# Masks of one head group added by TensorE, a bias fold in four steps, a packed ring, and new places for all instruction streams

## The chip, the cores and the metric

The kernel runs on one core of one Trainium2 chip. The metric is the device time of one execution in microseconds (us). The time of the kernel before is the median of three executions.

## The reference, cut to what matters

Two layers run one after the other on x (4 x 1024 x 512, float32) with a context of 4 x 64 x 512.

```python
# layer 0: transformer block, 16 heads of 32, note scores / (32 ** -0.5)
xn1 = ln(x, g1, be1)
x = x + mha(xn1, xn1, Wq_s.., causal=True) @ W1 + b1      # self attention, 1024 x 1024 scores, 4 batches x 16 heads
xn2 = ln(x, g2, be2)
x = x + mha(xn2, ctx, Wq_c.., causal=False) @ W2 + b2     # cross attention, 64 keys
x = x + relu(ln(x, g3, be3) @ Wf1 + bf1) @ Wf2 + bf2      # 512 -> 2048 -> 512
# layer 1: three rounds of routing weights (softmax over the sequence), a sigmoid gate and a layer norm
```

What the change touches is the causal self attention and the passage from it to the cross attention.

## The kernel before, in words

The self attention is cut into 16 head groups g (batch g // 4, four heads each), and a group into two halves c2 of 512 queries. A group needs:

- projections (`pj`, lines 55 to 57): each product is three fp32r matmuls of high and low parts; ScalarE writes the high part (`pjh`, L879), VectorE the low one (`pjl`, L1013), and DMAs (`stack`, L603) put them into the stacked operands `qs` and `ks`.
- a pass for the row maxima (`mx`): scores in rows of queries by TensorE (L766), masked and reduced by VectorE (L1027 with the mask where a tile meets the diagonal, L1031 without). `mxT` (L779) turns the maxima, `tq` (L889) writes them into a row of `qs`, and `tqd` (L609) copies this row to the other three heads by a DMA.
- the attention proper: `sc` (L809) computes 128 keys x up to 512 queries. Where a tile meets the diagonal, `low` (L1038, VectorE) adds a 128x128 mask in PSUM; then `ex` (L922, ScalarE) writes the exponentials, for the first key tile into `es`, for the others into a ring `er` of 8 slots of 512. GpSimd adds them up (L681), TensorE multiplies them with the values (`pv`, L821). Per group there are 32 `low` and 64 `ex`.
- the division: `fin` (L830, L933), `f0` to `f3d` (L613, L1047, L617, L623, L687, L628).

Seven PSUM banks are handed out in the order of the planned ends. For batches 1 to 3 a layer norm (`ld`, `st`, `nm`, `lnT`..) runs some groups ahead; its last part falls into groups 1 to 2, 5 to 6 and 9 to 10.

The order of the work on every engine is written out by hand: `order1()` gives each step a place in units of one group (place 14.3 is 30% into group 14), all steps are sorted by place, and each engine's program walks this one list. So a place decides order alone; semaphores decide the times. The places of group g come from tables with one row for each of four groups (`r = g % 4`), with special rows for groups 0 and 1. SyncE issues all DMAs, in the same order, and waits in its turn.

Into groups 14 and 15, which have no projections of a later group to compute, `order2()` puts the preparation of the cross attention: weights are loaded (`2ld`, L1175; `2kv`, L1182), split by ScalarE and VectorE (`2wh`, L1349 to L1355; `2wl`, L1418), the norm's shift is folded into a bias (`2wb`, L1251: 16 fp32 matmuls of one column, 32 passes in the trace), keys and values of the context are made (`2ck`, L1259; `2cv`, L1268), zeroes are written by GpSimd (`2z`, L1214, L1217), and the first chunk of 512 queries starts (`2ldc`, L1197; `2sh`, L1371; `2w1`). From place `CROSS_AT` on, 8 chunks of the cross attention follow with a fixed pattern, and then the third stage, whose places are counted from the end of the second.

Of the kernel before, what the change touches and what calls it, by code (L numbers as in the profile page):

```python
# [14 lines left out]
KT = 4  # L15
# [106 lines left out]
LN_LOAD = (-2.514, -2.024, -1.712, -1.56)  # L122
LN_TURN = (-2.071, -1.822, -1.573, -1.348)
CUT = (0.292, 0.27, 0.283, 0.294)
PROJ_0 = (27.2, 31.3, 37.9, 40.4)
PROJ_1 = (-1.329, -1.236, -1.109, -1.047)
PROJ = ((-1.661, -1.491, -1.269, -1.082), (-1.853, -1.456, -1.346, -1.171), (-1.872, -1.647, -1.316, -1.202), (-1.958, -1.475, -1.34, -1.21))
PROJ_LONG = (0.067, 0.08, 0.146, 0.146)
VALUES_0 = (40.2, 52.3, 66.7, 68.9)
VALUES = ((-1.149, -0.992, -0.719, -0.081), (-1.444, -1.08, -0.796, -0.377))  # L130
VALUES_LONG = 0.1
MAX_0 = -0.007
MAX_1 = (-0.809, -0.507, -0.024)
MAX = ((-1.031, -0.726, -0.051), (-1.012, -0.739, -0.002), (-1.033, -0.705, -0.043), (-0.988, -0.72, -0.05))


def order1():
# [19 lines left out]
    for b in range(1, NB):  # L157
        for qt in range(4):
            t += ln_times(b, qt, 4 * b + LN_LOAD[qt], 4 * b + LN_TURN[qt])
    for g in range(16):  # L160
        r = g % 4
        cut = CUT[r]
        at = [at0(a) for a in PROJ_0] if g == 0 else [g + a for a in (PROJ_1 if g == 1 else PROJ[r])]
        for c2 in range(2):
            for wq in range(2):
                n = 2 * c2 + wq
                t += proj_times(g, c2, wq, at[n], at[n] + (0.05 if g < 2 else PROJ_LONG[r]))
                back = g - 2 + (CUT[(g - 2) % 4] if n == 0 else CUT[(g - 2) % 4] + (1 - CUT[(g - 2) % 4]) * 0.54 if n == 1 else 1) + 0.03
                t.append((at[n] + 0.1 if g == 0 else max(at[n] + PROJ_LONG[r] + 0.07, back), ("stack", g, c2, wq)))
        if g % 2 == 0:  # L170
            for sp in range(4):
                s, d = (at0(VALUES_0[sp]), 0.05) if g == 0 else (g + VALUES[r // 2][sp], VALUES_LONG)
                t += spread(s, s + d, [(("vm", g // 2, sp, i), 1) for i in range(4)])
                t.append((s + d, ("ve", g // 2, sp)))
        m0, m1, end = (at0(46), at0(54), MAX_0) if g == 0 else [g + a for a in (MAX_1 if g == 1 else MAX[r])]
# [54 lines left out]
CROSS_AT = 16.793  # L230
CROSS_LOAD = (14.019, 14.431, 14.754, 14.309, 15.318)
CROSS_SPLIT = (14.581, 14.853, 15.576)
CROSS_ONCE = (14.168, 15.027, 14.983, 15.099, 14.261, 15.089, 15.146, 14.946)
CROSS_KEYS = (15.173, 15.19, 15.199, 15.461, 15.405)
CROSS_0 = (15.723, 15.776, 15.812, 16.19)


def order2():
# [5 lines left out]
    t = list(zip(CROSS_ONCE, (("2kc",), ("2kb",), ("2wb",), ("2bw",), ("2z", 2), ("2z", 0), ("2z", 1), ("2cd",))))  # L244
# [102 lines left out]
def program(nc, A, out):  # L347
    top = ExitStack()
    with top:
# [89 lines left out]
        Q.useA, Q.useP, Q.useM, Q.useS, Q.outS, Q.slot, Q.pv = {}, {}, {}, {}, {}, {}, {}  # L439
        for s in O1:  # L440
# [10 lines left out]
            if s[0] == "sc" and s[3]:  # L451
                Q.slot[s[1:]] = len(Q.slot)
            if s[0] == "pv":
                for i in range(4):
                    Q.pv[s[1:] + (i,)] = len(Q.pv)
        Q.slot_of = {at: k for k, at in Q.slot.items()}

# [16 lines left out]
        s_sao, s_rcp, s_rec, s_low = sem("s_sao"), sem("s_rcp"), sem("s_rec"), sem("s_low")  # L474

# [59 lines left out]
        def x_rows(b, qt, i):  # L535

            return Q.xr[:, i, :] if b else Q.v[:, 2 * qt + i, :]

# [95 lines left out]
        def pool1(e, w):  # L634
# [6 lines left out]
            for s in O1:  # L641
# [28 lines left out]
                elif s[0] == "pv" and s[3]:  # L670
                    _, g, c2, j = s
                    off = max(0, 128 * (j - 4 * c2))
                    for i in range(4):
                        at = Q.slot[g, c2, j, i]
                        es, er = Q.esum[c2][i][:, off:512], Q.er[:, at % 8, off:512]
# [13 lines left out]
        def pe1(e, w):  # L689
# [10 lines left out]
            for s in O1:  # L700
# [95 lines left out]
                elif s[0] == "sc":  # L796
# [10 lines left out]
                    if par:  # L807
                        w.wait_ge(d_oh1, 16)
                    t = e.matmul(ps[:, off:512], Q.ks[par][0:100, i, 128 * j:128 * j + 128],  # L809
                                 Q.qs[par][0:100, i, 512 * c2 + off:512 * c2 + 512], start=True, stop=True)  # L810
                    t.then_inc(s_fillS.sem, 1)
                elif s[0] == "pv":
                    _, g, c2, j = s
                    nj, off = 4 * c2 + 4, max(0, 128 * (j - 4 * c2))
                    for i in range(4):
# [3 lines left out]
                        src = Q.er[:, Q.slot[g, c2, j, i] % 8, :] if j else Q.esum[c2][i][:]  # L819
                        h = 128 * (g % 2) + 32 * i  # L820
                        e.matmul(bank[BO][32 * i:32 * i + 32, off:512], values(g)[:, j, h:h + 32], src[:, off:512],  # L821
# [11 lines left out]
        def act1(e, w):  # L833
            w.wait_ge(d_cols, 16)
            for s in O1:
# [21 lines left out]
                elif s[0] == "nm":  # L857
# [4 lines left out]
                                 scale=sm[:, 104 + i:105 + i]).then_inc(s_nrm.sem, 1)  # L862
                elif s[0] == "lnh":
# [37 lines left out]
                elif s[0] == "ex":  # L901
                    _, g, c2, j, i = s
                    off, n = max(0, 128 * (j - 4 * c2)), 2 * g + c2
                    if j >= 4 * c2:
                        w.wait_ge(s_low, 32 * g + 4 * j + i + 1)
                    else:
                        w.wait_ge(s_fillS, Q.useS["sc", g, c2, j, i] + 1)
                    if j:
                        at = Q.slot[g, c2, j, i]
                        dst = Q.er[:, at % 8, off:512]  # L910
                        if at >= 8:
                            w.wait_ge(s_add, at - 7)
                            w.wait_ge(s_pv, Q.pv[Q.slot_of[at - 8]] + 1)
# [331 lines left out]
        def pe2(e, w, s):  # L1245
            if s[0] == "2wb":
                freeK(w, 0)
                w.wait_ge(d_raw2[1], 64)
                for m in range(4):
                    for k in range(KT):  # L1250
                        t = e.matmul(bank[0][:, m:m + 1], R.raw[1][:, k, 128 * m:128 * m + 128], col("be2", k), start=k == 0, stop=k == 3)  # L1251
                t.then_inc(s_fillK.sem, 1)
# [930 lines left out]
```

## Time and profile before

| | |
|---|---|
| time, median of 3 (lowest to highest) | 2273.32 us (2270.26 to 2276.59) |
| profiled execution, its own time | 2272.72 us |
| its span in the trace | 2270.9 us |
| mean granted TensorE clock | 0.984 of full speed |
| PE (TensorE) busy | 2161.4 us, 95% of the span |
| VectorE, ScalarE, GpSimd busy | 61%, 38%, 41% |

Group g of the self attention can be told in the trace by the copy of its result at its end (L929): group 9 is about 583 to 635 us, group 10 635 to 692, group 13 796 to 848, group 14 848 to 906, group 15 906 to 970. The cross attention lasts to about 1420 us, the third stage to the end. In part 2 of the page each digit is a fortieth of the span, 57 us, about one group. A busy PE is not PE at its peak: a matmul whose clock is halved is busy for twice as long.

### The profile page before, as it was taken

How to read it: one execution, taken by the hardware profiler on the slowest of the kernel's cores; microseconds unless marked ns; L12 is line 12 of the kernel's file. 1: busy time of each engine (PE TensorE's matmuls, PEld its weight loads, DVE VectorE, ACT ScalarE, POOL GpSimd, SP SyncE). 2: the span in 40 equal slices, each digit the busy share in tenths (PEclk: the TensorE clock that was granted, in tenths of full speed). 3: DMA queues.
4: the chain of work that ended last, by engine and by line, in shares of the span. 5: the costliest groups of instructions: out<-in, count | busy, mean ns of one | idle time of the engine just before them, and what ended most of it. 6: DMA issues, size and time to landing. Idle time of an engine off the chain costs nothing.

```text
span 2270.9 us, 32174 instructions
## 1 busy us (share of the span) xinstructions
PE 2161.4 (95%) x11590; PEld 1604.5 (71%) x11590; DVE 1395.7 (61%) x3349; ACT 868.7 (38%) x1610; POOL 932.4 (41%) x943
## 2 busy tenths in 40 slices
PE   7999999999999998889999998999999999999996
PEld 5666666666656664467777776888887887888784
DVE  5577766876786676456666677543455636455546
ACT  4156555655565555534333433221221222121213
POOL 1068767777777778643333342101020202111112
PEclk9999999999999997999999999999999999999998
DMA  7655555555564564211122121320112121121101
GB/s 234 78 82 97 93 85 87 106 89 83 91 111 76 82 96 126 71 56 56 56 70 77 63 80 42 121 84 24 61 61 82 53 74 66 65 66 56 42 33 47
DMA packets 106324, 177.34 MB, mean 78 GB/s; under 512 B 18335, under 2 KB 23455, under 8 KB 106161
## 3 DMA queue, kind: packets, MB, share of 16 engines
q1 hardware_dynamic: 106164, 175.29, 33.1%
q8 instruction: 91, 1.49, 0.3%
q14 instruction: 69, 0.56, 0.1%
HBM read 83.67 MB, written 40.13 MB: 55 GB/s over the span
## 4 chain that ended last, share of the span: by engine, by line
PE 81%; DVE 7%; ACT 5%; issue 3%; POOL 2%; DMA 1%; SPq 0%; POOLq 0%; ACTq 0%; DVEq 0%
PE psum L55 19%; PE psum L56 18%; PE psum L57 18%; PE psum L821 6%; PE psum L766 6%; PE psum L809 5%; PE psum L724 1%; DVE psum L1027 1%; ACT sx L1377 1%; PE psum L830 1%; PE psum L743 1%; PE psum L1327 1%; DMA small<-es 1%; PE psum L1319 1%; PE psum L1268 1%
## 5 line engine op out<-in xcount | busy, mean ns | idle before, releaser
L681 POOL TENSOR_TENSOR es<-es,er 128x512 f32<-128x512 f32 (+3 forms) x640 | 588.0, 959 | 258.4 <-PE psum L821 243.6
L922 ACT ACTIVATE er<-psum 128x512 f32<-128x512 f32 (+3 forms) x640 | 278.4, 471 | 285.6 <-DVE psum L1038 176.2
L1027 DVE CUSTOM_DVE_ANT_0 psum<-psum,mask_ts 128x384 f32<-128x384 f32 (+3 forms) x512 | 249.4, 502 | 152.9 <-PE psum L766 150.6
L766 PE MATMUL psum<-ks,qs 96*128 96x512 f32 (+3 forms) x768 | 260.4, 371 | 7.4 <-DVE mx L1027 3.5
L809 PE MATMUL psum<-qs,ks 100*128 100x512 f32 (+3 forms) x768 | 252.0, 365 | 10.6 <-DVE mx L1027 5.1
L1876 ACT ACTIVATE fy<-psum,cols 128x512 f32<-128x512 f32 x128 | 88.2, 689 | 451.9 <-PE psum L57 451.4
L766 PEld LDWEIGHTS psum<-ks,qs 96*128 96x128 f32 x768 | 139.7, 191 | 115.2 <-issue 32.9
L1031 DVE TENSOR_REDUCE mx<-psum 128x1 fp32r<-128x512 f32 x256 | 175.6, 686 | 61.0 <-PE psum L766 60.0
L55 PE MATMUL psum<-fh,hh 128*128 128x512 f32 x512 | 201.0, 393 | 7.1 <-DVE hl L1977 7.1
L55 PE MATMUL psum<-fah,fh 128*128 128x512 f32 x512 | 202.9, 396 | 0.0
L1975 DVE CAST hh<-fy 128x512 fp32r<-128x512 f32 x128 | 61.2, 478 | 228.5 <-ACT fy L1876 228.1
L57 PE MATMUL psum<-fah,fl 128*128 128x512 f32 x512 | 200.1, 391 | 0.0
L56 PE MATMUL psum<-fal,fh 128*128 128x512 f32 x512 | 199.9, 390 | 0.0
L57 PE MATMUL psum<-fh,hl 128*128 128x512 f32 x512 | 199.4, 389 | 0.0
L56 PE MATMUL psum<-fl,hh 128*128 128x512 f32 x512 | 199.3, 389 | 0.0
L809 PEld LDWEIGHTS psum<-qs,ks 100*128 100x128 f32 x768 | 143.5, 194 | 58.3 <-DVE mx L1027 17.6
L1242 POOL TENSOR_TENSOR pp<-pp,small 128x1024 f32<-128x1024 f32 x32 | 61.2, 1912 | 265.9 <-DVE small L1507 265.9
L1772 POOL TENSOR_TENSOR et<-et,vpb 128x512 f32<-128x512 f32 x24 | 35.5, 1477 | 284.9 <-ACT et L1902 284.9
L1038 DVE TENSOR_TENSOR psum<-psum,mask_st 128x128 f32<-128x128 f32 x512 | 138.3, 304 | 22.7 <-PE psum L809 21.8
L821 PE MATMUL psum<-er,v 128*32 128x512 f32 (+3 forms) x1280 | 138.5, 488 | 0.7 <-ACT er L922 0.4
L55 PEld LDWEIGHTS psum<-fh,hh 128*128 128x128 f32 x512 | 96.1, 188 | 28.8 <-DVE hl L1977 9.3
L57 PEld LDWEIGHTS psum<-fah,fl 128*128 128x128 f32 x512 | 96.3, 188 | 20.6
(260 smaller groups left out, 4588.7 us busy)
## 6 DMA issues: line engine op xcount, KB each, us to landing
qs<-stage SPq DMA_DIRECT2D x96, 256.0 KB, 5.7
ks<-stage SPq DMA_DIRECT2D x96, 256.0 KB, 8.3
rs<-rs_d SPq DMA_DIRECT2D x32, 256.0 KB
sa_d<-rs SPq DMA_DIRECT2D x32, 256.0 KB, 2.1
sx<-sa_d SPq DMA_DIRECT2D x8, 1024.0 KB, 5.7
xt<-in_x SPq DMA_DIRECT2D x32, 256.0 KB, 6.0
x_d<-xt SPq DMA_DIRECT2D x32, 256.0 KB, 2.0
fw<-in_Wf SPq DMA_DIRECT2D x16, 512.0 KB, 5.3
```

The source lines that it names most:

```text
L55: e.matmul(dst, lh, rh, start=start, stop=False)
L56: e.matmul(dst, lh, rl, start=False, stop=False)
L57: return e.matmul(dst, ll, rh, start=False, stop=stop)
L681: e.tensor_tensor(es, es, er, ALU.add).then_inc(s_add.sem, 1)
L766: t = e.matmul(bank1(*s)[:, v * wd:v * wd + wd], Q.qs[par][0:96, i, 128 * ti:128 * ti + 128], Q.ks[par][0:96, i, c0:c0 + wd], start=True, ...
L809: t = e.matmul(ps[:, off:512], Q.ks[par][0:100, i, 128 * j:128 * j + 128], Q.qs[par][0:100, i, 512 * c2 + off:512 * c2 + 512], start=True, ...
L821: e.matmul(bank[BO][32 * i:32 * i + 32, off:512], values(g)[:, j, h:h + 32], src[:, off:512], start=j == 0, stop=j == nj - 1).then_inc(s_p ...
L922: e.activation(dst, bank1("sc", g, c2, j, i)[:, off:512], ACT.Exp, scale=SCALE).then_inc(s_freeS.sem, 1)
L1027: t = e.tensor_tensor_reduce(out=ps, in0=ps, in1=mask_ts[:, 512 - wd:512], scale=1.0, scalar=-3e38, op0=ALU.add, op1=ALU.max, accum_out=mx ...
L1031: e.tensor_reduce(mx[:, at:at + 1], bank1(*s)[:, 0:wd], AX, ALU.max).then_inc(s_red.sem, 1)
L1038: e.tensor_tensor(ps, ps, mask_st[:], ALU.add).then_inc(s_low.sem, 1)
L1876: e.activation(y[:], ring3(("h", c, m)), ACT.Relu, bias=col("bf1", m), scale=1.0).then_inc(s_r3.sem, 1)
```

## The change

Five things are changed.

1. In group 14 (`MASKED_BY_PE`) VectorE adds no masks for `ex`. Instead, after each of the 32 score matmuls of the diagonal TensorE multiplies the unit matrix with a copy of the mask (`mask_r`, fp32r, in the place of the value weights, which are no longer needed) into the same 128 columns. `ex` then waits for TensorE and not for VectorE. One ScalarE step (`mkr`, at 13.78) makes the copy.
2. The bias fold `2wb` becomes four steps with places 0.034 apart.
3. The ring `er` has the same 4096 elements, but a piece takes only as many as it has columns (512, 384, 256 or 128); `freed_by` gives the last piece that lay there.
4. The tables have twelve rows: groups 0 to 3, groups 4 to 11 (two by two), groups 12 to 15.
5. The places are new. The max pass of every group is some 0.073 later; projections, layer norm and values are moved by under 0.12, those of group 0 by up to 3.7 us on its own scale; the cuts of groups 14 and 10 differ. The weight splits of the cross attention are 0.129 and 0.085 earlier, their first load 0.119 later, `CROSS_AT` is 0.149 earlier, the first chunk 0.016 later.

```diff
-PROJ_1 = (-1.329, -1.236, -1.109, -1.047)
...
-VALUES = ((-1.149, -0.992, -0.719, -0.081), (-1.444, -1.08, -0.796, -0.377))
...
-MAX_1 = (-0.809, -0.507, -0.024)
-MAX = ((-1.031, -0.726, -0.051), (-1.012, -0.739, -0.002), (-1.033, -0.705, -0.043), (-0.988, -0.72, -0.05))
+LN_LOAD = ((-2.516, -2.026, -1.714, -1.561), (-2.557, -2.032, -1.746, -1.568), (-2.517, -2.027, -1.83, -1.563))
+CUT = (0.292, 0.27, 0.283, 0.294, 0.292, 0.27, 0.283, 0.295, 0.292, 0.27, 0.317, 0.294)
...
+MAX = ((-0.985, -0.652, 0.023), (-0.735, -0.433, 0.05), (-0.966, -0.596, 0.031), (-0.914, -0.646, 0.024),
+       (-0.957, -0.652, 0.023), (-1.01, -0.666, 0.071), (-0.959, -0.631, 0.031), (-0.914, -0.646, 0.037), ...
+       (-0.959, -0.565, 0.108), (-0.919, -0.646, 0.024))
+def row(g, n=4):
+    return g if g < n else n + g % n if g < 3 * n else g - n
+MASKED_BY_PE = (14,)
...
-CROSS_AT = 16.793
-CROSS_LOAD = (14.019, 14.431, 14.754, 14.309, 15.318)
-CROSS_SPLIT = (14.581, 14.853, 15.576)
-CROSS_KEYS = (15.173, 15.19, 15.199, 15.461, 15.405)
-CROSS_0 = (15.723, 15.776, 15.812, 16.19)
+CROSS_AT = 16.644
+CROSS_LOAD = (14.138, 14.447, 14.77, 14.325, 15.345)
+CROSS_SPLIT = (14.452, 14.768, 15.491)
+CROSS_FOLD = 0.034
+CROSS_KEYS = (15.174, 15.191, 15.2, 15.432, 15.406)
+CROSS_0 = (15.739, 15.792, 15.83, 16.206)
...
-                if s[0] == "sc" and s[3] >= 4 * c2 :
+                if s[0] == "sc" and s[3] >= 4 * c2 and g not in MASKED_BY_PE:
                     t += [(a + 0.014, ("low", *s[1:])), (a + 0.028, ("ex", *s[1:]))]
                 elif s[0] == "sc":
                     t.append((a + 0.001, ("ex", *s[1:])))
...
+    t.append((MASKED_BY_PE[0] - 0.22, ("mkr",)))
...
+        for at, (g, c2, j, i) in Q.slot_of.items():
+            width = 512 - max(0, 128 * (j - 4 * c2))
+            pos = 0 if pos + width > 4096 else pos
+            under = [n for n, (lo, hi) in held.items() if lo < pos + width and pos < hi]
+            Q.freed_by[at] = max(under, default=None)
...
-                                 Q.qs[par][0:100, i, 512 * c2 + off:512 * c2 + 512], start=True, stop=True)
+                                 Q.qs[par][0:100, i, 512 * c2 + off:512 * c2 + 512], start=True, stop=not diag)
+                    if diag:
+                        w.wait_ge(s_mkr, 1)
+                        t = e.matmul(ps[:, off:off + 128], identr[:], mask_r(), start=False, stop=True)
...
+                elif s[0] == "mkr":
+                    w.wait_ge(s_const, 6)
+                    w.wait_ge(s_fillA, Q.useA["vm", 7, 3] + 1)
+                    e.activation(mask_r(), mask_st[:], ACT.Copy).then_inc(s_mkr.sem, 1)
...
+                if j == 2:
+                    w.wait_ge(s_fillS, read(MASKED_BY_PE[-1], 1, 1))
```

## Rows read from the trace of the kernel before

**Rows 1.** The page, parts 1, 2, 4 and 5.

```profile
PE 2161.4 (95%) x11590; PEld 1604.5 (71%) x11590; DVE 1395.7 (61%) x3349; ACT 868.7 (38%) x1610; POOL 932.4 (41%) x943
...
PEclk9999999999999997999999999999999999999998
...
PE 81%; DVE 7%; ACT 5%; issue 3%; POOL 2%; DMA 1%; SPq 0%; POOLq 0%; ACTq 0%; DVEq 0%
...
L922 ACT ACTIVATE er<-psum 128x512 f32<-128x512 f32 (+3 forms) x640 | 278.4, 471 | 285.6 <-DVE psum L1038 176.2 <-PE psum L809 89.5 <-POOL es L681 9.5
```

**Rows 2.** Busy time of each engine by group, then granted clock, DMA share, GB/s.

```profile
424.00:479.00 55.00, 52.55 (x321) 33.86 (x321) 44.21 (x152) 35.13 (x72) 40.39 (x47) 1.00 0.57 106
...
583.00:635.00 52.00, 51.84 (x329) 34.86 (x329) 38.54 (x126) 30.49 (x66) 40.26 (x45) 1.00 0.57 90
635.00:692.00 57.00, 53.99 (x325) 35.30 (x324) 44.85 (x154) 35.76 (x73) 41.40 (x49) 0.97 0.55 107
...
848.00:906.00 58.00, 51.91 (x246) 28.35 (x246) 39.79 (x132) 33.30 (x71) 47.88 (x48) 0.79 0.55 132
906.00:970.00 64.00, 57.81 (x257) 29.25 (x255) 30.85 (x73) 36.76 (x80) 41.48 (x39) 0.90 0.19 63
```

**Rows 3.** The same view, short stretches of groups 14 and 15.

```profile
875.00:880.00 5.00, 3.81 (x15) 1.24 (x13) 3.99 (x11) 4.22 (x8) 5.00 (x5) 0.80 0.35 114
880.00:885.00 5.00, 4.93 (x14) 2.68 (x10) 3.69 (x11) 1.14 (x3) 5.00 (x5) 0.50 0.27 91
...
890.00:895.00 5.00, 2.88 (x13) 1.46 (x13) 3.34 (x10) 3.97 (x10) 5.00 (x7) 0.66 0.24 82
...
900.00:905.00 5.00, 5.00 (x31) 4.61 (x31) 0.00 (x0) 0.19 (x1) 5.00 (x2) 0.50 0.00 0
...
950.00:960.00 10.00, 6.60 (x23) 3.35 (x19) 7.12 (x9) 4.89 (x9) 6.46 (x5) 0.51 0.46 177
```

**Rows 4.** ScalarE's waits in group 14: us in total, times, longest.

```profile
ACT er L922 <- DVE psum L1038: 13.0, 12, 3.4
```

**Rows 5.** Busy time of the masks (L1038) in groups 9 and 14.

```profile
583.00:635.00 52.00, 8.45 (x32) 1.00 0.57 90
...
848.00:906.00 58.00, 9.13 (x33) 0.79 0.55 132
```

**Rows 6.** PE in order of time: the fold; the start's fold; four matmuls of 128 columns.

```profile
896.64 6.99 PE L1251 MATMUL psum<-cols,raw 128*128 128x1 f32 x32
...
60.74 0.95 PE L733 MATMUL psum<-cols,er 128*128 128x1 f32 x8
...
600.66 0.49 PE L779 MATMUL psum<-ident,mx 128*100 128x128 f32 x4
```

**Rows 7.** GpSimd in order of time, group 14.

```profile
873.02 18.69 POOL L681 TENSOR_TENSOR es<-es,er 128x512 f32<-128x512 f32 x16
...
899.53 3.52 POOL L1217 MEMSET kbh<- 128x4096 f32 x1
902.98 3.52 POOL L1217 MEMSET kbl<- 128x4096 f32 x1
```

**Rows 8.** DMAs of group 14: count, KB each, median us to landing.

```profile
raw<-in_W SPq DMA_DIRECT2D x7, 256.0 KB, 2.9
```

**Rows 9.** TensorE's weight loads, what they waited for in group 15.

```profile
PEld psum L809 <- DVE W2l L1418: 2.5, 2, 2.1
```

**Rows 10.** The chain of waits, pieces in order of time: start, us, what.

```profile
851.73 9.33 DMA small<-es
...
947.26 5.48 DMA sx<-sa_d
...
980.06 3.40 PE psum L1286 x16
```

**Rows 11.** Group 9 in order of time: the copy of the maxima, the first score of the second half.

```profile
586.79 0.71 SPq L609 DMA_DIRECT2D qs<-qs  x1
...
598.43 0.39 PE L809 MATMUL psum<-qs,ks 100*128 100x512 f32 x1
```

More of the change, by code:

```diff
@@ L158, in order1 @@
         for qt in range(4):
-            t += ln_times(b, qt, 4 * b + LN_LOAD[qt], 4 * b + LN_TURN[qt])
+            t += ln_times(b, qt, 4 * b + LN_LOAD[b - 1][qt], 4 * b + LN_TURN[b - 1][qt])
     for g in range(16):
-        r = g % 4
+        r = row(g)
         cut = CUT[r]
-        at = [at0(a) for a in PROJ_0] if g == 0 else [g + a for a in (PROJ_1 if g == 1 else PROJ[r])]
+        at = [at0(a) for a in PROJ_0] if g == 0 else [g + a for a in PROJ[r]]
         for c2 in range(2):
@@ L243, in order2 @@
     at2 = lambda n: X0 + T * n if n < 28 else E + 0.82 * T * (n - 28)
-    t = list(zip(CROSS_ONCE, (("2kc",), ("2kb",), ("2wb",), ("2bw",), ("2z", 2), ("2z", 0), ("2z", 1), ("2cd",))))
+    t = [(CROSS_ONCE[2] + CROSS_FOLD * m, ("2wb", m)) for m in range(4)]
+    t += list(zip(CROSS_ONCE[:2] + CROSS_ONCE[3:], (("2kc",), ("2kb",), ("2bw",), ("2z", 2), ("2z", 0), ("2z", 1), ("2cd",))))
     for k in range(KT):
@@ L438, in program @@
         O1 = [s for _, s in O1]
-        Q.useA, Q.useP, Q.useM, Q.useS, Q.outS, Q.slot, Q.pv = {}, {}, {}, {}, {}, {}, {}
+        Q.useA, Q.useP, Q.useM, Q.useS, Q.outS, Q.slot, Q.pv, Q.low = {}, {}, {}, {}, {}, {}, {}, {}
         for s in O1:
@@ L452, in program @@
                 Q.slot[s[1:]] = len(Q.slot)
+            if s[0] == "low":
+                Q.low[s[1:]] = len(Q.low)
             if s[0] == "pv":
@@ L456, in program @@
         Q.slot_of = {at: k for k, at in Q.slot.items()}
+        Q.piece, Q.freed_by, held, pos = {}, {}, {}, 0
+        for at, (g, c2, j, i) in Q.slot_of.items():
[3 more added lines that the diff above has]
+            Q.freed_by[at] = max(under, default=None)
+            for n in under:
+                lo, hi = held.pop(n)
+                if hi > pos + width:
+                    held[n] = pos + width, hi
+            Q.piece[at] = slice(pos, pos + width)
+            pos += width
+            held[at] = Q.piece[at].start, pos
         d_rows, d_ct0, d_wv0, d_wt0, d_wg0, d_out0 = (sem(n) for n in ("d_rows", "d_ct0", "d_wv0", "d_wt0", "d_wg0", "d_out0"))
@@ L474, in program @@
         s_sao, s_rcp, s_rec, s_low = sem("s_sao"), sem("s_rcp"), sem("s_rec"), sem("s_low")
+        s_mkr = sem("s_mkr")
         def stk(par, w, c2):
@@ L537, in x_rows, with mask_r, exps @@
             return Q.xr[:, i, :] if b else Q.v[:, 2 * qt + i, :]
+        def mask_r():
+            return Q.W["v"][0][:, 0, 0:128]
+        def exps(at):
+            return Q.er[:].rearrange("p a n -> p (a n)")[:, Q.piece[at]]
         def raw1(j):
@@ L674, in pool1 @@
                         at = Q.slot[g, c2, j, i]
[L675 removed]
+                        es, er = Q.esum[c2][i][:, off:512], exps(at)
                         if j == 1:
@@ L818, in pe1 @@
                         w.wait_ge(s_sao, 2 * g + c2)
-                        src = Q.er[:, Q.slot[g, c2, j, i] % 8, :] if j else Q.esum[c2][i][:]
+                        src = exps(Q.slot[g, c2, j, i]) if j else Q.esum[c2][i][:]
                         h = 128 * (g % 2) + 32 * i
-                        e.matmul(bank[BO][32 * i:32 * i + 32, off:512], values(g)[:, j, h:h + 32], src[:, off:512],
+                        e.matmul(bank[BO][32 * i:32 * i + 32, off:512], values(g)[:, j, h:h + 32], src,
                                  start=j == 0, stop=j == nj - 1).then_inc(s_pv.sem, 1)
@@ L903, in act1 @@
                     off, n = max(0, 128 * (j - 4 * c2)), 2 * g + c2
-                    if j >= 4 * c2:
-                        w.wait_ge(s_low, 32 * g + 4 * j + i + 1)
+                    if j >= 4 * c2 and g not in MASKED_BY_PE:
+                        w.wait_ge(s_low, Q.low[g, c2, j, i] + 1)
                     else:
@@ L909, in act1 @@
                         at = Q.slot[g, c2, j, i]
[L910 to L913, printed above, removed]
+                        dst, last = exps(at), Q.freed_by[at]
+                        if last is not None:
+                            w.wait_ge(s_add, last + 1)
+                            w.wait_ge(s_pv, Q.pv[Q.slot_of[last]] + 1)
                         else:
@@ L1246, in pe2 @@
             if s[0] == "2wb":
[L1247 to L1252, printed above, removed]
+                m = s[1]
+                if m == 0:
+                    freeK(w, 0)
+                    w.wait_ge(d_raw2[1], 64)
+                for k in range(KT):
+                    t = e.matmul(bank[0][:, m:m + 1], R.raw[1][:, k, 128 * m:128 * m + 128], col("be2", k), start=k == 0, stop=k == 3)
+                if m == 3:
+                    t.then_inc(s_fillK.sem, 1)
             elif s[0] == "2ck":
```

30 lines of the change are left out of this document (16 added, 14 removed).

## The prediction

> **What bounds the kernel now.** I read the page first. TensorE (PE) is busy for 95% of the span and the chain that ended last is PE for 81% [rows 1], so time can only come from PE's idle time, from PE work that goes, or from its clock. The granted clock is full nearly everywhere: the digits show one 7 in the sixteenth slice, which is group 14 [rows 1]. The busy time by group says where that sits. Group 9 has PE busy for 51.84 of 52 us with VectorE at 38.5; group 6 and its twin group 10, where a layer norm of the next batch is prepared, have 52.55 of 55 and 53.99 of 57; group 14 has 51.91 of 58 at a mean clock of 0.79, and group 15 57.81 of 64 at 0.90 [rows 2]. Group 14 has 246 matmuls where group 9 has 329, and takes 6 us more [rows 2]. So ordinary groups have nothing to give, and two stretches have: 14 and 15.
>
> A mean clock of 0.79 over 58 us is 0.21 x 58 / 0.5 = 24.4 us at half speed; 0.90 over 64 us is 12.8 us [rows 2]. The short stretches show how it comes. From 875 to 880 PE is busy for 3.81 of 5 us and the clock falls; at half speed PE is then busy for 4.93 of 5, it idles again (2.88 of 5 at 890), and for 900 to 905 it is full of work at half speed while VectorE does nothing [rows 3]. What PE waits for there is VectorE: ScalarE's exponentials stood 13.0 us for the masks, once for 3.4 us [rows 4], and VectorE serves 9.13 us of masks [rows 5] beside the maxima and eight splits of W1 and Wq_c. The block that fills 900 to 905 is the bias fold, 32 passes in one piece of 6.99 us [rows 6].
>
> By the Trainium skill ("TensorE: Matmul & The Clock Gate", Part 1) the slow clock is the state after idleness and work releases it. The trace agrees so far: the clock fell behind 3.81 busy of 5 us. The same section says that the gate's observation runs free of the program, so the place of a fall can differ between runs; then part of my clock terms would be luck. This changes no term, it is why I don't take the clock terms in full.
>
> **The change part by part.**
>
> *Masks in group 14.* VectorE loses 32 masks; group 9 prices 32 at 8.45 us [rows 5]. PE gets 32 matmuls of 128 columns. Four of that form take 0.49 us with their tail [rows 6]; without it I take 0.11 each, 3.5 us. Bounds: 3.9 us by the full row, and nothing if all fall into the 58 - 51.91 = 6.1 us in which PE idles now [rows 2]. I take 3.5. In return the chain score, mask, exponential loses its middle link, so banks come free earlier. Of the 6.1 us of PE idle I take half away: -3 (bounds 0 and -6). `mkr` is one small ScalarE step on an engine with 24 of 58 us free [rows 2]; the value projection that it waits for is placed 0.17 groups (9 us) before it: 0, with 1 us as the upper bound.
>
> *Clock in group 14.* In its 24.4 us at half speed PE is busy for about 85% (4.93, 2.88 and 5.00 of 5 us [rows 3], mean 0.85): 20.8 us, which would be 10.4 at full speed. The fold is part of this: at full clock 8 passes take 0.95 us [rows 6], four steps 3.8 us instead of 6.99, and between them scores can go to VectorE, which idles throughout the block [rows 3]. I take 80% of 10.4: -8.3 (bounds 0 and -10.4).
>
> Is another engine next? GpSimd is busy for 47.88 us in group 14 [rows 2], but 7.04 of it are two memsets behind the last sum [rows 7] that nobody needs for the next few us. 40.8 us remain, so GpSimd allows the group some 8 to 10 us. The W1 loads are placed later and their splits earlier: the last load is at 14.438, its split at 14.572, 0.134 groups or 7 us, against 2.9 us to landing [rows 8]. That fits if SyncE isn't held by the division's steps just before it; if it is, ScalarE stands with the exponentials behind it, 2 us at most by the same row less the slack, taken as 0. Group 14 in sum: -3 - 8.3 + 3.5 = -7.8.
>
> *Group 15.* Scores stood 2.5 us for W2's low parts [rows 9], because a bank is shared with them; the W2 split is 0.085 groups (4.6 us) earlier: -1.5 (0 to -2.5). The new wait of its third weight split, for the scores of group 14, stands 0.49 groups behind them: 0. Its 12.8 us at half speed cost PE work of about 0.66 x 10 + 2.8 = 9.4 us, so 4.7 us at most [rows 2, 3]. But the fall at 950 lies beside the first load of `sx`, 5.48 us on the chain [rows 10], which still waits for the context's values; these are placed only 0.029 groups earlier. I take a third: -1.5. Sum -3.
>
> *The passage to the cross attention.* `CROSS_AT` 0.149 earlier looks like 8 us and is worth nothing: the first chunk's steps keep their own places, the last of its query projection ends before 16.65, and nothing of group 15 but the division's last steps stands after that. The same steps are in the same order, and chunks 1 to 7 and stage three move as one piece. The normalisation before the first transposes of 980 us [rows 10] has no PE work to cover it before or after. 0 (-2 to +1).
>
> *The ring.* The pieces of the diagonal need 3072 of 4096 elements instead of 12 of 8 slots. ScalarE waits for GpSimd's sums for 9.5 us in the whole kernel [rows 1], mostly with PE busy. -0.5 (0 to -2).
>
> *The places of groups 0 to 13.* The max pass of each group is 0.073 groups (4 us) later against the scores. Group 9's PE is at 99.7% [rows 2], so such a group can only lose. In groups 2, 6 and 10 the layer norm's steps of VectorE now meet another part of the max pass; group 10 takes 2 us more than its twin and has a clock of 0.97 [rows 2], and it alone of them gets a later place for nothing but its loads (-1.83 for -1.712). I take -1.5 for group 10 and 0 for the rest (bounds -5 and +20, see the third rival). Start of the kernel: moves of up to 3.7 us on PE's own full queue, 0 (-2 to +2).
>
> Sum: -7.8 - 3 - 0.5 - 1.5 = -12.8, against the profiled execution's 2272.7 us (span 2270.9 and 1.8 around it): 2259.9. The median of the runs is 0.6 us above the profiled one: 2260.5, said as 2260.
>
> **The rivals.**
>
> *A: as above,* 2251 to 2266.
>
> *B: the clock falls anyway.* For: VectorE keeps 30 us in group 14 with the splits, now closer together, each 128x512; the `sx` load stays; 40.8 us of GpSimd in order; ScalarE has the splits' copies too. Then group 14 gains only the waits less the masks and some 3 us of clock: -3 + 3.5 - 3 - 1.5 (W2) = -4: 2269. Against: the longest waits of rows 4 are the masks themselves.
>
> *C: slower, by the later max pass.* The maxima of the second half end now 4 us later, up to 0.071 of a group inside the group that needs them. Place: the row copy L609 ahead of the first score of the second half. In group 9 it is issued at 586.79 and that score starts at 598.43, 11.6 us later [rows 11]. 4 us later, 7.7 remain, and a small DMA in this queue took 9.33 us in group 14 [rows 10]. That is 1.6 us of PE idle, which group 10 shows to be enough for a fall of the clock (57 for 55 us [rows 2]). Since groups repeat, 1.6 us in each of 13 is +21, net +8: 2281. It decides above 1 us per group. Against: the 9.33 us come from large transfers queued ahead; they don't move, so a copy issued later would wait less behind them.
>
> *D: more.* Clock kept in both groups in full and the layer norm groups relieved: -10.4 - 6 + 0 (masks inside idle time) - 4.7 - 2.5 - 3 = -27: 2246.
>
> *E: the change is what it says but without effect,* as groups 14 and 15 are held by GpSimd: that is B with less, 2272.
>
> **How the numbers follow.** 0.3% is 6.8 us: faster means below 2266.5, slower above 2280. A 0.60, B 0.15, C 0.12, D 0.08, E 0.05. Faster takes A but for a small part, D and a third of B: 0.57 + 0.08 + 0.05 = 0.70. Slower is C above 2280 and some B and C mixed, 0.09; the same 0.21. The range leaves out most of C and half of D: 2247 to 2275.
>
> **What would show it.** Right: clock digits of 9 or so in group 14's slice and a mean over 0.9 there; group 14 at 50 us, group 15 at 61; L1038 with 480 instructions; the fold as four pieces of about 1 us; ordinary groups within 0.2 us of 52, 55, 54 and 50. Wrong by B: half-speed stretches of 10 us still in group 14. Wrong by C: ordinary groups longer by one and the same amount, PE idle ahead of L809 at the start of the second half. The prediction fails if groups 1 to 13 together move by more than 5 us either way, or if the cross attention, which I hold to be the same, changes.

## The result, and the profile after

The changed kernel takes 2283.86 us (median of 4 runs, 2283.49 to 2285.35) against 2272.61 us of the kernel before in the same series: a ratio of 1.0049 with a 95% interval of 1.0034 to 1.0064, some 11 us slower. The forecast was 2260 us, 0.6% faster, in a range of 2247 to 2275: the sign is wrong, and the range was missed.

The page of the changed kernel, the parts that answer to [rows 1]:

```profile
PE 2165.1 (95%) x11622; PEld 1608.7 (71%) x11622; DVE 1401.3 (61%) x3317; ACT 866.9 (38%) x1611; POOL 931.4 (41%) x943
...
PEclk9999999999999997899999999999999999999998
```

ScalarE's exponentials in the groups by line (columns as in part 5 of the page):

```profile
L965 ACT ACTIVATE er<-psum 128x512 f32<-128x512 f32 (+3 forms) x640 | 278.4, 472 | 260.8 <-DVE psum L1081 158.6 <-PE psum L845 90.9 <-PE psum L849 6.0
```

The 32 added matmuls and the 32 masks that went are there. ScalarE's waits for GpSimd's sums fell from 9.5 us to 2.6 (too little for this line), and its idle time here fell from 285.6 to 260.8 us. Still the span is 10.8 us longer. TensorE's slices 16 and 17 have clock digits of 7 and 8 where before only one stood out.

I take the end of each half from the copy `sao<-psum` that ScalarE makes of its accumulators.

| stretch | before, us | after, us | difference |
|---|---|---|---|
| group 0 ends at | 160.8 | 158.4 | -2.4 |
| groups 1 to 13 | 687.1 | 691.6 | +4.5 |
| group 14 | 57.8 | 51.5 | -6.3 |
| group 15, first half | 16.6 | 32.6 | +16.0 |
| group 15, second half | 47.7 | 47.3 | -0.4 |
| what follows | | | -0.6 |

The loss sits in the first half of group 15. The busy times of groups 14 and 15, and of ten microseconds at their seam (columns as in [rows 2]):

```profile
850.00:902.00 52.00, 45.92 (x256) 25.61 (x255) 35.01 (x97) 33.26 (x71) 39.55 (x41) 0.86 0.61 141
902.00:981.00 79.00, 65.86 (x283) 36.57 (x281) 42.23 (x85) 37.10 (x81) 47.74 (x42) 0.81 0.18 59
902.00:912.00 10.00, 4.53 (x20) 4.15 (x18) 10.00 (x10) 0.05 (x1) 7.91 (x5) 0.50 0.22 59
```

Group 14 does what was hoped: VectorE has 35.01 us where it had 39.79, and the clock is 0.86 for 0.79. In group 15 the clock is 0.81 for 0.90, which over the longer stretch is 30 us at half speed for 12.8. In the ten microseconds VectorE is busy all the time with ten instructions, ScalarE does nothing, and TensorE has work for 4.53 us at half clock. What VectorE does there, in order of time:

```profile
899.11 0.70 DVE L1070 CUSTOM_DVE_ANT_0 psum<-psum,mask_ts 128x512 f32<-128x512 f32 x1 [0.22 <-PE psum L801]
899.73 0.14 DVE L1070 DVE_READ_ACCUMULATOR2_ANT mx<- 128x1 fp32r x1
899.73 11.74 DVE L1476 COPY pp<-ctc 128x256 f32<-128x256 f32 x8
911.39 0.68 DVE L1074 TENSOR_REDUCE mx<-psum 128x1 fp32r<-128x512 f32 x1
911.99 0.69 DVE L1070 CUSTOM_DVE_ANT_0 psum<-psum,mask_ts 128x512 f32<-128x512 f32 x1
```

Eight copies of the context, which take 0.28 us each when nothing holds them, last 11.74 us, and the first of them alone 10.33 us. No step of mine contains them. GpSimd beside them:

```profile
897.33 1.29 POOL L722 TENSOR_TENSOR rs<-sao,rs 128x512 f32<-128x512 f32 x1
898.58 4.44 POOL L716 TENSOR_TENSOR es<-es,er 128x256 f32<-128x256 f32 x8
902.94 3.52 POOL L1260 MEMSET kbh<- 128x4096 f32 x1
906.39 3.52 POOL L1260 MEMSET kbl<- 128x4096 f32 x1
```

GpSimd's instructions stand end to end until 909.91, and the first copy ends at 910.06. And TensorE (L1295 is the fold, L845 the scores, L814 the transposition of the maxima):

```profile
904.83 1.70 PE L1295 MATMUL psum<-cols,raw 128*128 128x1 f32 x8
912.12 0.79 PE L845 MATMUL psum<-qs,ks 100*128 100x512 f32 x1 [5.59 <-DVE mx L1074]
913.01 0.93 PE L814 MATMUL psum<-ident,mx 128*100 128x128 f32 x4
```

The two last maxima of the second half stand behind the copies on VectorE; the bank of one of them and the transposition of all of them stand behind these, and TensorE, which takes its steps in the order of the list, stands 5.59 us. Its clock is at half from 901.0 to 924.9; the fall came before TensorE stood still, so this stall did not begin it. Two lines of the waits between 896 and 940 us (us in total, times, longest) say the same for the other engines:

```profile
ACT es L965 <- DVE psum L1081: 11.1, 1, 11.1
...
PE psum L845 <- DVE mx L1074: 5.8, 2, 5.6
```

In the kernel before, the same copies took 3.19 us:

```profile
895.29 3.19 DVE L1429 COPY pp<-ctc 128x256 f32<-128x256 f32 x8
```

There GpSimd had a gap from 896.9 to 899.1 us, and the first copy (1.78 us) ended at that moment; its two memsets [rows 7] came at 899.53.

### The profile page after: what moved, and what is told of

Its sections match the earlier page's. It is cut to its first block, busy times and chain, and to the rows that moved or that the text cites. A ratio compares the mean times of both kernels' runs of the same rounds, so it can differ in the third digit from the quotient of the medians.

```text
span 2281.7 us, 32057 instructions
## 1 busy us (share of the span) xinstructions
PE 2165.1 (95%) x11622; PEld 1608.7 (71%) x11622; DVE 1401.3 (61%) x3317; ACT 866.9 (38%) x1611; POOL 931.4 (41%) x943
## 4 chain that ended last, share of the span: by engine, by line
PE 82%; DVE 6%; ACT 4%; issue 3%; DMA 2%; POOL 2%; SPq 0%; POOLq 0%; ACTq 0%; DVEq 0%
PE psum L55 19%; PE psum L56 18%; PE psum L57 18%; PE psum L801 6%; PE psum L860 6%; PE psum L845 5%; PE psum L759 1%; PE psum L869 1%; ACT sx L1424 1%; PE psum L1372 1%; PE psum L778 1%; PE psum L1364 1%; PE psum L1313 1%; DVE psum L1070 1%; ACT pT L1451 1%
## 5 line engine op out<-in xcount | busy, mean ns | idle before, releaser
L965 ACT ACTIVATE er<-psum 128x512 f32<-128x512 f32 (+3 forms) x640 | 278.4, 472 | 260.8 <-DVE psum L1081 158.6
L845 PE MATMUL psum<-qs,ks 100*128 100x512 f32 (+3 forms) x768 | 250.3, 366 | 16.1 <-DVE mx L1074 6.7
L845 PEld LDWEIGHTS psum<-qs,ks 100*128 100x128 f32 x768 | 143.0, 193 | 68.4 <-issue 12.6
L1081 DVE TENSOR_TENSOR psum<-psum,mask_st 128x128 f32<-128x128 f32 x480 | 128.6, 302 | 28.2 <-PE psum L845 27.8
```

The lines of the kernel that those rows point to most:

```text
L965: e.activation(dst, bank1("sc", g, c2, j, i)[:, off:512], ACT.Exp, scale=SCALE).then_inc(s_freeS.sem, 1)
L1081: e.tensor_tensor(ps, ps, mask_st[:], ALU.add).then_inc(s_low.sem, 1)
```

## The experiments

Theory H: VectorE's copies from SBUF to SBUF stand until GpSimd lets them in; the shorter group 14 brings them there while GpSimd is still in its sums with the memsets behind, and what stands behind the copies decides the price. Rivals: R, the fold in four pieces and the denser splits let the clock fall; M, the new places of groups 0 to 13 (the later max pass, rival C of the prediction). A ratio is that of a kernel's time to the time of the kernel before in the same series, with its 95% interval in brackets. Losses and gains below are differences of ratios times 2273 us, unless a profiled execution is named. With ten runs each such a difference is good to some 3 or 4 us either way.

**The copies on ScalarE, all else as changed.**

```diff
 # in scalar's step list, was in vector's
+elif s[0] == "2cd":
+    w.wait_ge(d_ct2, 16); stacked(w)
...
-    e.tensor_copy(dst[:, :, j, :], R.ct[:, k, :]...).then_inc(s_cd.sem, 1)
+    e.activation(dst[:, :, j, :], R.ct[:, k, :]..., ACT.Copy).then_inc(s_cd.sem, 1)
```

> The changed kernel, with the eight copies of the context (pp<-ctc) at the same place but on ScalarE instead of VectorE. Theory 1 (the loss is the copies on VectorE, which stand as long as GpSimd works without a gap): 11.7 us on VectorE become eight copies of some 0.4 us on ScalarE, the first half of group 15 falls from 32.6 us to 17 to 19, the half-speed stretch of 24 us behind it goes, and the time is 2268 to 2272, 12 to 16 us less than the changed kernel and slightly under the kernel before. Rival 1 (the first half of group 15 is long because the fold's steps and the masks' passes meet a slow clock): nothing moves, 2284. Rival 2 (the new places of groups 1 to 13 are the loss): 2284 less 2 at most.

Measured: 2275.65 us (10 runs), ratio 1.0013 [1.0000, 1.0025]: 8.2 us of the 11 come back, less than the 12 to 16 expected, and the kernel is still 3.0 us behind the kernel before. TensorE is at half clock from 906.4 to 916.7 us, 10 us for 24. The copies now take 0.41 us each beside the same GpSimd work, and the first half of group 15 takes 22.8 us instead of 32.6 (16.6 before):

```profile
901.92 2.56 ACT L1417 ACTIVATE pp<-ctc 128x256 f32<-128x256 f32 x8
```

**The memsets moved instead of the copies.** Behind the first four sums of group 15 in the changed kernel, and, in the kernel before, ahead of the last four sums of group 14.

```diff
-CROSS_ONCE = (14.168, 15.027, 14.983, 15.115, 14.261, 15.112, 15.146, 14.959)
+CROSS_ONCE = (14.168, 15.027, 14.983, 15.115, 14.261, 15.2, 15.205, 14.959)
 # kernel before
-CROSS_ONCE = (14.168, 15.027, 14.983, 15.099, 14.261, 15.089, 15.146, 14.946)
+CROSS_ONCE = (14.168, 15.027, 14.983, 15.099, 14.261, 14.965, 14.966, 14.946)
```

> The changed kernel, with GpSimd's two memsets of kbh and kbl (3.52 us each) behind the first four sums of group 15 instead of ahead of them. Theory 1: GpSimd has a gap once group 14's sums are done at about 903, so the first copy ends there and not at 910; the copies take about 5 us in all, the first half of group 15 gives back 6 to 10 us, and the time is 2274 to 2278, unless the keys of the context now wait for the zeroes. Rival 1: nothing before 915 us changes, 2284.

> The kernel before, with the same two memsets ahead of the last four sums of group 14. Nothing of the change is in it. Theory 1: the copies, which begin at 895.3, now meet GpSimd without a gap until the memsets and the sums behind them are done at about 905: the first copy takes 8 to 11 us instead of 1.8, the masks behind it on VectorE come late, and the first half of group 15 or the end of group 14 is 5 to 12 us longer: 2278 to 2285, the loss of the change without the change. Rival 1: the copies keep their 3.2 us and the time its 2273.

The first gave 2285.32 us (one run). The copies fell to 1.82 us as H says, but the time did not: a new wait came for the buffer that is now zeroed too late,

```profile
ACT kbh L1409 <- POOL kbl L1260: 9.7, 1, 9.7
```

so this run shows the release of the copies and nothing on their price. The second gave 2273.88 us (one run; the runs of the kernel before beside it lie between 2270.29 and 2278.58), no loss that one run can show where 5 to 12 us were expected, though its copies were held as long as those of the changed kernel:

```profile
892.47 11.67 DVE L1429 COPY pp<-ctc 128x256 f32<-128x256 f32 x8
904.06 0.29 DVE L1038 TENSOR_TENSOR psum<-psum,mask_st 128x128 f32<-128x128 f32 x1
```

TensorE beside and behind them:

```profile
893.83 6.99 PE L1251 MATMUL psum<-cols,raw 128*128 128x1 f32 x32
900.75 0.65 PE L821 MATMUL psum<-er,v 128*32 128x128 f32 x6
904.71 0.64 PE L821 MATMUL psum<-er,v 128*32 128x128 f32 x2 [3.31 <-ACT er L922]
```

Here H's price failed while its mechanism held. Behind the copies stands a mask, not a maximum, and beside them TensorE is in the undivided fold, which waits for nobody; it idles 3.31 us, and group 14 takes 59.8 us for 57.8. So a stall of 10 us need not cost 10 us: its price is set by what waits behind it, and by how much work TensorE has meanwhile.

**The masks of group 14: given back to VectorE, and as the only edit.**

```diff
 # changed kernel
-MASKED_BY_PE = (14,)
+MASKED_BY_PE = ()
 # kernel before, alone
+MASKED_BY_PE = (14,)
...
+                    if diag:
+                        t = e.matmul(ps[:, off:off + 128], identr[:], mask_r(), start=False, stop=True)
```

> The changed kernel without its first part: group 14's masks are added by VectorE again, all places and the rest of the change as they are. Theory 1: VectorE has 8.5 us more work in group 14, which is then 54 to 58 us instead of 51.5; it comes to the copies later, when GpSimd may or may not be at the memsets, so the first half of group 15 is anything from 17 us (GpSimd idle) to 30. Time 2272 to 2290. Rival 1 (the masks' passes are themselves the cost): under 2280 with a short first half of group 15.

> The kernel before with the first part of the change alone: group 14's masks by TensorE, all places, the ring and the fold as before. Theory 2 (the masks part is a gain, since the changed kernel without it was 8 us slower): VectorE's 8.5 us go, group 14 falls from 57.8 to 50 to 54 us, group 15 stays near 64, as VectorE comes to the context's copies only after its maxima; time 2264 to 2270. Rival (the 8 us came only from where the clock fell): 2270 to 2276.

The first: 2292.17 us (4 runs), 1.0077 [1.0060, 1.0094], 6 us slower than the changed kernel. The masks by TensorE are a gain, and the slower group 14 doesn't avoid the stall either: its GpSimd work is later too (copies 907.53 to 916.90 us). The second: 2276.31 us (10 runs), 1.0014 [1.0005, 1.0024], slower than before. Group 14 falls from 57.8 to 47.4 us and the first half of group 15 rises from 16.6 to 28.3:

```profile
891.71 15.58 DVE L1448 COPY pp<-ctc 128x256 f32<-128x256 f32 x8
907.21 0.68 DVE L1437 TENSOR_TENSOR Wq_cl<-psum,Wq_ch 128x512 fp32r<-128x512 f32 x1
```

The first copy takes 14.17 us, up to 905.88; GpSimd's second memset ends at 905.7. This one part of the change alone, on the old places, makes the stall. Neither expectation held.

TensorE in the same run (L1268 is the fold, L819 the scores):

```profile
892.25 3.90 PE L1268 MATMUL psum<-cols,raw 128*128 128x1 f32 x32
907.94 1.54 PE L819 MATMUL psum<-qs,ks 100*128 100x512 f32 x3 [9.39 <-DVE Wq_cl L1437]
```

Here no maximum stands behind the copies; the last one was done at 890.5. TensorE stands 9.39 us for a PSUM bank that the split of Wq_c behind the copies must read first. The fold is undivided as in the run with the early memsets, but it met the full clock, took 3.90 us for 6.99, and was over at 896.2, so it covered less. That this is what makes the one stall dear and the other cheap is read from the two traces; no run isolates it.

**The copies on ScalarE without and with the masks, on the kernel before.**

```diff
 # control: only "2cd" from vector's to scalar's steps
 # both: the same and
+MASKED_BY_PE = (14,)
```

> The kernel before with the copies of the context on ScalarE and nothing else, the control of e10. There the first copy stood for only 1.8 us and VectorE had an idle time of 6.4 us right behind: Theory 1: 2271 to 2274, no change. Rival (the copies on VectorE always cost): under 2269.

> The kernel before with two edits: group 14's masks by TensorE (as in e5, 2276.3 us) and the copies of the context on ScalarE. In e5 the copies held VectorE for 15.6 us, and group 14 took 47.4 us and group 15 76.8 (57.8 and 64.3 in the kernel before). Theory 1: without the stall group 15 is back at 64 to 66, the two groups take 112 to 116 us for 122, and the time is 2263 to 2268: faster than both kernels. Rival (the gain of group 14 is only work put off into group 15): 2272 to 2276.

The control gave 2272.87 us (10 runs), 0.9996 [0.9984, 1.0009]: the move itself is worth nothing that can be measured in the kernel before. Both together gave 2268.29 us (12 runs), 0.9975 [0.9962, 0.9987], 8.9 us better than the masks alone. It beats both kernels and is the best of this study, at the slow end of the 2263 to 2268 expected. Its groups 14 and 15 take 51.0 and 64.6 us:

```profile
852.00:903.00 51.00, 47.14 (x268) 28.41 (x268) 29.56 (x83) 34.31 (x77) 43.54 (x44) 0.90 0.58 146
903.00:968.00 65.00, 58.43 (x258) 29.82 (x258) 31.16 (x74) 37.40 (x82) 45.28 (x41) 0.90 0.19 62
```

**Other places for VectorE's copies in the changed kernel.**

```diff
-CROSS_ONCE = (14.168, 15.027, 14.983, 15.115, 14.261, 15.112, 15.146, 14.959)
+CROSS_ONCE = (14.168, 15.027, 14.983, 15.115, 14.261, 15.112, 15.146, 15.026)
 # and, in the other kernel, 14.90
```

> The changed kernel with the copies still on VectorE but behind the last maxima of group 15 (place 15.026 for 14.959). They will still stand until GpSimd's memsets end, some 8 us. Theory 1b (the stall costs what stands behind it: in the changed kernel two maxima, whose transposition holds TensorE's queue; in e3, with nothing behind, a stall of 9.5 us cost 1 us): the transposition is done before, only masks wait; 3 to 8 us less than the changed kernel, 2276 to 2281. Theory 1a (every stall of the copies costs the same): 2284.

> The changed kernel with the copies still on VectorE but earlier, at 14.90 for 14.959, so some 4 us sooner. Theory 1 (a copy stands until GpSimd has a gap, not until the instruction at hand ends): the first copy starts at about 896 and still ends with the memsets at about 910, 13 to 14 us, with three maxima behind it; 2284 to 2290. Rival (it waits for one instruction of GpSimd, 0.5 to 3.5 us): the copies take under 5 us and the time is 2274 to 2278.

Behind the last maxima: 2281.51 us (5 runs), 1.0037 [1.0024, 1.0050], 2.7 us better, with intervals that overlap; the first copy takes 3.71 us, up to the end of the memsets at 908.0. Earlier: 2283.80 us (one run); the first copy takes 7.42 us and ends at 901.6, where GpSimd has its next gap (sooner than the 910 expected), and group 14 pays with 60.7 us what group 15 gets back (73.1). No place on VectorE tried here was free.

**The fold: in one block, and in four.**

```diff
 # copies on ScalarE, else as changed
-    t = [(CROSS_ONCE[2] + CROSS_FOLD * m, ("2wb", m)) for m in range(4)]
+    t = [(CROSS_ONCE[2] + 0.0000001 * m, ("2wb", m)) for m in range(4)]
 # masks and scalar copies on the kernel before
+    t = [(CROSS_ONCE[2] + 0.034 * m, ("2wb", m)) for m in range(4)]
```

> The changed kernel with the copies on ScalarE (as in e1, 2275.7 us) and the bias fold as one block at its old place 14.983. My prediction's view (one block stalls VectorE and holds the clock low): 2 to 5 us slower than e1, 2278 to 2281, with the clock at half for longer around it. Rival (the four steps stand between the first scores of group 15 and delay them in a stretch at half speed, three steps of 1.3 to 1.9 us): 1 to 4 us faster than e1.

> e10 (the kernel before, masks of group 14 by TensorE, copies on ScalarE; 2268.3 us) with the bias fold in four steps at 14.983 and 0.034 apart. My prediction (the block holds the clock low): 2264 to 2267. The view after e7: three of four steps stand between the first scores of group 15, no gain, 2268 to 2271.

2274.58 us (10 runs), 1.0002 [0.9993, 1.0012], against the 1.0013 with four pieces; and 2271.84 us (11 runs), 0.9988 [0.9979, 0.9996], against the 0.9975 with one. Two kernels of the experiments on the places (below) also differ in the fold alone: 1.0004 with four pieces, 0.9994 with one. The fold in four steps looks dearer by 2.5, 3.0 and 2.3 us in three surroundings, each time with intervals that overlap, so a cost of that size is likely and not shown; what is excluded is a gain of the size that I forecast. In the profiled executions the first half of group 15 moves the same way in all three: from 18.9 to 22.8, from 16.8 to 21.3 and from 18.9 to 22.8 us.

**The ring alone.** The edit is the diff's for the ring and nothing else, on the kernel before.

> The kernel before with the packed ring and nothing else. Prediction: -0.5 us, 2271 to 2274, ScalarE's waits for GpSimd's sums (9.5 us in the kernel before) fall by half. Rival (GpSimd works in fewer pieces without gaps, and VectorE's copies meet it otherwise): 2275 or more.

2273.26 us (10 runs), 0.9997 [0.9985, 1.0010]. ScalarE's waits for GpSimd fall from 9.5 to 1.1 us, and it buys nothing that can be measured.

**The places.** First the copies on ScalarE and groups 0 to 13 as before, else as changed (14 and 15 new); then, on masks, scalar copies, ring and one fold, three choices: groups 0 to 13 new; the cross places with groups 14 and 15 new; the cross places alone. (In all four the projections and values of group 14 have their new places, and where groups 0 to 13 are new and 14 isn't, group 14's first max pass begins later too, since it can't begin inside group 13's.)

```diff
 # example: the last of them against the one before it
-CUT = (..., 0.317, 0.294)
+CUT = (..., 0.283, 0.294)
-MAX = (..., (-0.959, -0.565, 0.108), (-0.919, -0.646, 0.024))
+MAX = (..., (-1.033, -0.705, -0.043), (-0.988, -0.72, -0.05))
```

> The changed kernel with the copies on ScalarE (as in e1, 2275.7 us) and with the places of groups 0 to 13 as in the kernel before. Theory 3 (the new places of groups 1 to 13 cost 4.5 us, those of group 0 gain 2): groups 1 to 13 take 52.5, 54.6, 54.3, 49.6 us again, time 2271 to 2275. Rival (clock falls alone): no difference, or one of both signs within 2 us.

> e10 (2268.3 us) with the packed ring and the new places of groups 0 to 13, the later max pass among them (group 14's max pass begins 0.113 later, since it can't begin inside group 13's); the rest as before. By the groups' periods in the traces (691 us for groups 1 to 13 against 686, less 2 in group 0) 2269 to 2273. Rival (it is the clock alone): 2268.

> e10 (2268.3 us) with the packed ring and the new places of groups 14 and 15 and of the cross attention; groups 0 to 13 and the fold in one block as before. If these places cost the rest: 2272 to 2275, as in e6 (2273.9), which has the fold in four. If the fold cost it: 2268 to 2270.

> As f2, but cut and max pass of groups 14 and 15 as before too, so that (but for small moves of the projections of 14 and 15) only the places of the cross attention's preparation are new: splits of W1, Wq_c and W2 earlier, the first load later. If the later max pass of groups 14 and 15 is what costs in f2: 2267 to 2270. If the earlier splits cost (VectorE has them inside the maxima of group 15): as f2.

Measured: 2273.90 us (10 runs), 1.0004 [0.9992, 1.0016], 2 us better than with the new places; groups 1 to 13 take 685.4 us for 690.7. New places of 0 to 13: 2269.24 us (9 runs), 0.9983 [0.9973, 0.9993], 1.8 us worse than without. Both differences are smaller than their error. Cross with 14 and 15: 2273.39 us (12 runs), 0.9994 [0.9983, 1.0006], 4.3 us worse. Cross alone: 2278.80 us (12 runs), 1.0018 [1.0005, 1.0031], 9.8 us worse, more than either expectation had. The waits in its groups 14 and 15:

```profile
PEld psum L801 <- ACT er L965: 9.4, 6, 5.1
PE psum L801 <- ACT er L965: 4.8, 1, 4.8
...
ACT W1h L1400 <- DMA raw<-in_W: 3.9, 1, 3.9
DVE W1l L1472 <- ACT psum L1402: 3.8, 1, 3.8
```

ScalarE comes to a split of W1 before the raw weight has landed, stands 3.9 us with the exponentials behind it, and TensorE has 0.49 us of work between 870 and 875. Its clock falls there, to 0.65 from 875 us to the end of the group, and group 14 takes 61.0 us for 51.0. That the 9.8 us are this wait and this clock is read from the trace; no run took the wait away alone. This is the risk that I named at "2 us at most, taken as 0". With the new places of 14 and 15 beside it the changed kernel itself has only 0.2 us of that wait in group 14. What the 4.3 us of the new cross, 14 and 15 places are was not tried apart, but the trace of the changed kernel shows one candidate, and it is the mechanism of rival C. The row copy of the maxima for the second half of group 14 (L644) is issued at 857.52, and the first score that needs it waits for it:

```profile
857.52 0.68 SPq L644 DMA_DIRECT2D qs<-qs  x1
864.83 1.22 PE L845 MATMUL psum<-qs,ks 100*128 100x512 f32 x2 [2.79 <-DMA qs<-qs]
```

In the kernel before, that copy was issued at 848.62, the score started at 859.39, and TensorE's wait there was 0.4 us at most. TensorE's clock is at half from 863.4 to 870.3. Of the four kernels of this experiment the two with the new max pass of group 14 have this wait with 2.9 us, the other two with 0.9 and 0.7.

**The sum of the parts.** From the masks with scalar copies, -5.7 us: the fold in four +3.0, the ring about 0, the places of 0 to 13 +1.8, those of 14, 15 and the cross +4.3, together +3.4; measured for the kernel with all of these, the first experiment, +3.0. Each part is uncertain by about 3 us, so an agreement within 0.4 is partly luck. The last part, the copies on VectorE, is the difference of the first experiment to the changed kernel itself: +8.2.

## Why the prediction was wrong

**The failed step is the sum of group 15 (-3; profiled execution +15.6).** It took the passage from group 14 to 15 as W2's split and the clock at `sx`, and left out the copies of the context, an unchanged step of VectorE. Their row was not read. Beside it I wrote that the two memsets are those "that nobody needs for the next few us" and that GpSimd allows the group 8 to 10 us. Nobody needs their results, but VectorE needs GpSimd out of the way. That step gave group 14 the very time that GpSimd's sums and memsets then took from VectorE. Shown by exchange: -8.2 us with only the copies moved off VectorE, -8.9 us on the old places, nothing measurable (0.9996) where the masks are not taken away. Whether the later max pass has a part in this price is open: in the changed kernel two maxima stand behind the copies, and the copies put behind them cost 2.7 us less, with intervals that overlap; on the old places no maximum stands there, and the stall costs as much.

The copies are not the whole miss. From -12.8 forecast to +11.2 measured it is 24 us, and they are 8.2 of them. The rest, by the experiments: masks, clock and fold -5.7 + 3.0 = -2.7 for -7.8, which is 5 us; the new places of groups 14, 15 and of the cross attention +4.3, where I had -3 for group 15, 7 us; groups 0 to 13 +1.8 for -1.5, 3 us; the ring 0.5. Of these only the loss by the new places of 14, 15 and the cross is near to clear of the noise by itself. One part of it was forecast in kind: TensorE's 2.79 us for the row copy at the second half of group 14 are rival C's wait, where I had put the new places of group 14 at nothing.

By the Trainium skill ("SBUF — State Buffer", Who interferes with whom) a plain copy of VectorE can take the pair of ports that it shares with GpSimd; whichever of the two is first has the pair to itself and the other waits, while ScalarE never waits. The trace agrees: the first copy was held on VectorE for 3.71 to 14.17 us in five kernels, and took 0.41 us on ScalarE beside the same sums. The same section of the Trainium skill has the lock last for one instruction; here the first copy stood through nine of GpSimd's, each at most 3.52 us, so the measured wait is longer than that rule gives. Nothing in the diff touches the copies, and that is why this rule has to be held against the steps that a change leaves alone too.

Step by step:

- *Masks in group 14 (-3 and +3.5) and the clock (-8.3), in sum -7.8.* Group 14 gave -6.3 in the profiled execution, but only -3.3 in two others of the same program up to the seam (54.5 us), so part of the 6.3 is luck. Masks with the stall removed give -5.7 [-8.6, -3.0], masks back on VectorE +6. The direction is right: masks off VectorE shorten group 14. The clock term was too large: group 14 still has 0.86, or 14.6 us at half speed, where I wanted over 0.9. The fold's 6.99 - 3.8 us were part of that term.
- *The fold in four* failed: taken for a gain (6.99 to 3.8 us), it gave none and by three comparisons cost 2.3 to 3, each within the noise. In the changed kernel the pieces took 0.95, 1.70, 1.70 and 1.87 us, 6.2 in all, as all but the first met the slow clock. Undivided it took 3.90 us where it met the full clock, so the 6.99 us were the clock's and not the block's. Why cutting should cost is argued only: scores between the pieces don't help when VectorE can't take them, and a block of 7 us covers a stall of its neighbours. All three comparisons have the copies on ScalarE, so it isn't the copies' stall.
- *W1 loads later, splits earlier (0, up to 2)*: too small a bound. The new cross places alone have a wait of 3.9 us for the raw weight and cost 9.8 us; in the whole change the wait is 0.2 us.
- *The ring (-0.5)*: right, 0 within its interval; the wait went (9.5 to 1.1 us) and was worth nothing that can be measured.
- *Groups 0 to 13 (-1.5, and rival C's +21)*: +2.1 in the profile, +1.8 and +2.0 in two comparisons. The gain isn't there, nor is C in these groups: TensorE waits 0.4 us for row copies in them, and they aren't longer by one amount (group 5 takes 54.0 us for 52.5, group 8 49.1 for 49.6, group 9 52.7 for 52.5). Group 10, which was to lose its excess of 2 us, has 58.6 for 56.2. Its new load place, -1.83 for -1.712, is an earlier one; I had read it as later.
- *The passage to the cross attention (0)*: right. From the end of group 15 to the cross attention's second chunk 26.0 us for 25.2, and what follows group 15 is 0.6 us shorter, for all that `CROSS_AT` is 0.149 earlier.
- *W2's low parts (-1.5) and the clock at `sx` (-1.5)*: right in direction. TensorE's weight loads wait 1.4 us for W2's low parts where they waited 2.5, and the half-speed stretch there is 6.8 us for 10.2. Together with the rest the second half of group 15 gained 0.4.

Of the rivals B (2269) was nearest in kind, as the clock did fall; but none put the stall on VectorE. Rival C, 2281, comes within 3 us of the measured time by luck: it summed 1.6 us over 13 ordinary groups, where its wait isn't, and its wait is 2.79 us in group 14, where only a part of the loss sits.

## What to carry to other kernels

When a stage is made shorter, list every step at its seam that the change leaves alone, and look at what runs beside it on the other engines: here an untouched copy of VectorE moved into GpSimd's busy stretch. The price of a stall is what stands behind it in its queue, less what the other engines can do meanwhile: a first copy held for 10.3 us cost 8.2 with two maxima behind it, one held for 14.2 us cost 8.9 with a weight split that kept a PSUM bank, and one held for 9.5 us beside a long fold at half clock cost nothing that its one run shows. So read the next rows, of the stalled engine and of TensorE, before giving it a number. Plain copies from SBUF to SBUF beside a busy GpSimd are better placed on ScalarE if it has time; in both kernels tried it had.

## What the runs showed of the hardware

A copy on VectorE waits for GpSimd over several instructions: 10.33 us over nine of them, 14.17 us over thirteen, 7.42 us over eleven additions and multiplications up to a gap, 3.71 us up to the end of a memset, which reads nothing. In two runs the two engines also took turns. With the memsets early in the kernel before, the first copy was released at 901.9 us, the end of the second memset, and three more took 0.54 us each beside sums of 0.50 us. With the masks back on VectorE the first copy began while GpSimd was idle, the next two took 0.56 and 0.54 us beside sums of 0.50, and the fourth stood 7.43 us, to the end of the second memset. What decides between the two was not found.

The place where the clock falls isn't fixed by the program. The changed kernel, the one with the copies on ScalarE and the one with its memsets later are the same program up to the copies at the end of group 14, and have 51.5, 54.5 and 54.5 us for group 14 and 58.6, 56.9 and 57.9 for group 10, and single runs of one program with masks and scalar copies lie between 2265.22 and 2273.07 us. Differences of 2 us therefore want ten runs, and a profiled execution alone does not show them.
